# Graph attention on one core: GpSimd multiplies three tiles of V per block, ScalarE sums the K·Q products of two

## The reference

```python
edge_index = jnp.stack([src, dst])
q = (x @ Wq + bq).reshape(n, H, DK)       # H = 8 heads, DK = 64
k = (x @ Wk + bk).reshape(n, H, DK)
v = (x @ Wv + bv).reshape(n, H, DK)
logits = jnp.einsum('ehd,ehd->eh', q[rows] * scale, k[cols]) + att_bias
row_max = jax.ops.segment_max(logits, rows, num_segments=n)
p = jnp.exp(logits - row_max[rows])
denom = jax.ops.segment_sum(p, rows, num_segments=n)
att = p / denom[rows]
y = jax.ops.segment_sum(att[:, :, None] * v[cols], rows, num_segments=n)
out = y.reshape(n, H * DK) @ Wo + bo
```

## Time and profile before

| | us |
|---|---|
| median of 3 runs | 3242.53 |
| lowest, highest | 3241.57, 3242.64 |
| the profiled execution, its own time | 3243.5 |
| its span, first to last instruction | 3241.7 |

### The profile page before, as it was taken

How to read it: one execution, slowest core, us unless ns; L and a number is a source line. 1 busy time by engine, 2 the same in 40 slices (tenths; PEclk the granted TensorE clock), 3 DMA queues, 4 the chain that set the end, 5 groups by cost and what they waited for, 6 DMA issues and landing times.

```text
span 3241.7 us, 62767 instructions
## 1 busy us (share of the span) xinstructions
PE 2890.7 (89%) x11939; PEld 1687.3 (52%) x11939; DVE 2847.3 (88%) x20435; ACT 2108.6 (65%) x7365; POOL 2263.5 (70%) x2562
## 2 busy tenths in 40 slices
PE   4899888888888278999999999999999999989998
PEld 3555554454555134555555555555555555554444
DVE  8997777767777378999999999999999999998887
ACT  8332222222222037999999999999999999974444
POOL 0477777777777746888888888888888888861121
PEclk6798899988888688999999999999999999999999
DMA  6343443433333487888888888888888888841222
GB/s 189 78 138 108 106 112 108 114 103 99 109 108 97 132 312 247 270 263 268 261 270 266 265 265 265 269 265 261 271 265 266 264 265 269 262 142 61 84 79 71
DMA packets 259601, 619.75 MB, mean 191 GB/s; under 512 B 62433, under 2 KB 80493, under 8 KB 258958
## 3 DMA queue, kind: packets, MB, share of 16 engines
q0 software_dynamic: 144832, 443.72, 43.6%
q1 hardware_dynamic: 110862, 164.95, 17.0%
q10 hardware_dynamic: 3520, 7.08, 0.6%
HBM read 553.68 MB, written 61.92 MB: 190 GB/s over the span
## 4 chain that ended last, share of the span: by engine, by line
DVE 46%; POOL 23%; issue 14%; PE 12%; DMA 2%; DVEq 1%; ACT 1%; SPq 0%; POOLq 0%
DVE big L1361 26%; POOL rec_scratch L673 23%; DVE big L1470 12%; PE banks L2024 5%; PE banks L2089 2%; DVEq L1470 1%; DVE big L1081 1%; DVE big L1455 1%; PE banks L2003 1%; PE banks L2012 1%; PE banks L1947 1%; DMA big<-kv_scratch,small 1%; DVE ext L1439 1%; PE banks L2092 1%; DMA big<-in_edge_attr_dram 1%
## 5 line engine op out<-in xcount | busy, mean ns | idle before, releaser
L886 ACT ACTIVATE big<-big,small 128x65 f32<-128x65 f32 x6164 | 1508.8, 340 | 5.1 <-DMA big<-kv_scratch,small 0.4
L1361 DVE SCALAR_TENSOR_TENSOR big<-banks,big 128x64 f32<-128x64 f32 x6656 | 1030.6, 214 | 35.8 <-PE banks L1947 18.0
L694 POOL DMA_INDIRECT big<-kv_scratch,small x832 | 844.5, 1015 | 280.7 <-DVE big L1361 133.0
L673 POOL DMA_INDIRECT rec_scratch<-big,small x782 | 773.7, 989 | 324.5 <-issue 237.9
L1947 PE MATMUL banks<-big,small 128*128 x1664 | 892.7, 619 | 44.2 <-DVE big L1361 35.0
L2003 PE MATMUL banks<-big,small 128*128 128x260 f32 x3328 | 882.9, 388 | 44.3 <-DVE big L1470 22.1
L2003 PEld LDWEIGHTS banks<-big,small 128*128 128x128 f32 x3328 | 616.3, 190 | 449.7 <-issue 289.9
L1470 DVE SCALAR_TENSOR_TENSOR big<-big,loS,banks 128x520 f32 x832 | 619.6, 745 | 6.3 <-PE banks L2003 4.1
L1838 PE MATMUL banks<-big 128*128 128x512 f32 (+1 forms) x1176 | 598.0, 656 | 22.2 <-DVE big L1071 22.2
L702 POOL TENSOR_SCALAR small<-iotaF,small 128x128 f32<-128x128 f32 x832 | 527.9, 635 | 65.8 <-PE banks L2003 39.0
L1361 DVE DVE_READ_ACCUMULATOR big<-banks,big 128x1 f32 x6656 | 522.7, 79 | 0.1
(11 more groups left out here) (274 smaller groups left out, 2733.7 us busy)
## 6 DMA issues: line engine op xcount, KB each, us to landing
rowR<-lo_rows SPq DMA_DIRECT2D x97, 256.0 KB
big<-src_rows SPq DMA_DIRECT2D x97, 256.0 KB
big<-in_x_dram SPq DMA_DIRECT2D x96, 256.0 KB, 4.1
big<-kv_scratch,small POOLq DMA_INDIRECT x832, 5.3
rec_scratch<-big,small POOLq DMA_INDIRECT x782
kv_scratch<-big SPq DMA_DIRECT2D x48, 260.0 KB
q_scratch<-big SPq DMA_DIRECT2D x48, 256.0 KB
kv_scratch<-big SPq DMA_DIRECT2D x48, 256.0 KB
```

Of the source, the lines that this page charges most:

```text
L673: e.indirect_dma_start(recd, bass.IndirectOffsetOnAxis(ap=ridx[:, c % 4, j:j + 1], axis=0), rec[:, 8 * c + j, :], None).then_inc(s_sc[c % ...
L694: e.indirect_dma_start(KV[:, vat(t):vat(t) + YW + D], None, KVd, bass.IndirectOffsetOnAxis(ap=recB[b_ % 4][:, t % 16, 9:10].bitcast(i32), ...
L886: ins = e.activation(heads(Vr(t), h, h + 1), heads(Vr(t), h, h + 1), ACT.Copy, scale=ph[:, h:h + 1])
L1361: ins = e.scalar_tensor_tensor(k_, QB[t % 2][:, 64 * h:64 * h + 64], 1.0, k_, ALU.mult, ALU.mult, accum_out=Lr[t // 16 % 2][:, t % 16, h:h ...
```

## The change

`on_pool` now names tiles 6, 10 and 14 of each block instead of tile 10 alone. POOL multiplies V of such a tile in step s = t+25, right ahead of the tile's one-hot, where before it was four steps earlier and behind a one-hot. ACT leaves these tiles out, so it has no `pva` in steps 13, 1 and 5.

For tiles 3 and 9 of each block (`summed`; 99 tiles) DVE multiplies K by Q with one instruction of 512 columns and no sums. ACT makes the sums with the new `sums(t)`: eight copies in place of 64 columns with an accumulator output, in step t+3 (steps 6 and 12), ahead of the `pva` of that step. `gather(s)` now waits also for the sums of tile s-5, since it writes over that product; the block's `lb` (adding the bias) waits for them too. The semaphore that counts the sums is `s_ab` taken on from the sorting.

```diff
-        on_pool = [t % 16 in (10,) and t < LAST for t in range(T)]
+        summed = [t % 16 in (3, 9) and t < LAST - 16 for t in range(T)]
+        sum_at = [sum(summed[:t + 1]) for t in range(T)]
+        s_sum, sum_base = s_ab, 2 * NCH
+        on_pool = [t % 16 in (6, 10, 14) and t < LAST for t in range(T)]
...
                 q.wait_ge(s_rd, k + 1)
+                if k >= 0:
+                    q.wait_ge(s_sum, sum_base + sum_at[k])
                 q.wait_ge(s_yt, v + 1)
...
                 if s - DEL - 2 >= 0:
+                    if on_pool[s - DEL - 2]:
+                        pvp(s - DEL - 2)
                     one_hot(s - DEL - 2)
-                if 0 <= s - DEL + 2 < T and on_pool[s - DEL + 2]:
-                    pvp(s - DEL + 2)
...
+            def sums(t):
+
+                q.wait_ge(s_rd, t + 1)
+                q.wait_ge(s_x2, t // 16 - 1)
+                for h in range(8):
+                    k_ = Kr(t)[:, 64 * h:64 * h + 64]
+                    ins = e.activation(k_, k_, ACT.Copy, accum_out=Lr[t // 16 % 2][:, t % 16, h:h + 1])
+                ins.then_inc(s_sum, 1)
...
+                if 3 <= s < T + 3 and summed[s - 3]:
+                    sums(s - 3)
                 if s >= DEL and not on_pool[s - DEL]:
                     pva(s - DEL)
...
+                if summed[t]:
+                    if not half:
+                        e.tensor_tensor(Kr(t), QB[t % 2], Kr(t), ALU.mult).then_inc(s_rd, 1)
+                    return
...
                 q.wait_ge(s_rd, 16 * b_ + 16)
+                q.wait_ge(s_sum, sum_base + sum_at[16 * b_ + 15])
```

## The result

The changed kernel takes 3441.51 us (median of four runs, 3438.78 to 3446.75), beside 3242.05 for the kernel before in the same comparison: 1.062 times, 95% interval 1.061 to 1.063. It is slower, as forecast, and 45 us beyond the forecast of 3396 us. The profiled execution has a span of 3440.3 us.

What follows compares the result with a forecast made beforehand. DVE bounds the kernel, with ACT and PE within 4%. The ring's terms sum to 35.95 us a block against 32.7, +3.2 us over 48 blocks, 154 us on 3243.5, giving 3396 us by the median; range 3265 to 3480 us.

Steps and rivals of the forecast that it cites:

- The bound and the mechanism: DVE full before; afterwards tile 14's gather waits for ACT's sums of tile 9, a 2.4 us stall against 1.1 saved.
- 3 or 4: Sign in the profile: ACT's wait ahead of the copy of one-hots stays or grows to 3 or 4 us a block.
- the ring: Chain from one gather of tile 14 to the next through POOL, DVE, PE and ACT: 35.95 us a block against 32.7.
- gather 14 to gather 0: POOL's steps from gather 14 to 15 (1.84 us) and 15 to 0 (2.85 us, with a product of V): 4.7 us.
- gather 0 to tile 0: Landing of gather 0, after which DVE starts tile 0: 5.3 us.
- tile 0's start to tile 2's end: DVE from the start of tile 0 to the end of tile 2: 5.65 us.
- from there to gather 14, with both sums: Via PE to ACT's step 4 3.05 us, ACT to step 12 15.1, tile 9's sums 1.95, semaphore 0.2.
- the pointer that is not read: ACT's sums priced like `pva`, which reads a pointer where sums have an accumulator: 0.243 us a head, 1.95 a tile.
- The lag of ACT behind tile 9: ACT starts the sums 3.35 us after tile 9's product, 4.4 us with DVE 1.1 us ahead by its savings.
- rival "not slower": ACT's sums come in time; POOL's 32.5 us bounds a block, 3230 us, or DVE's 31.6, 3189 us; chance 0.10.
- The length of the sums enters twice: Tile 3's and tile 9's sums lie on one ACT stretch: at 1.2 us a tile a block takes 34.4, at 2.7 37.4.
- ACT is never idle up to step 12: From the copy of step 4 ACT works without waits, 15.1 us to step 12, `pva` 5 exchanged for tile 3's sums.

Runs made afterwards that it cites:

- e5: Changed kernel, but ACT sums tile 3 in step 5 and tile 9 in step 10 instead of 6 and 12; 1.013 times the kernel before, block 33.7 us.
- e1: Changed kernel without sums on ACT, so only POOL's three products of V a block; 1.026 times the kernel before, block 34.6 us.
- e4: Changed kernel, but POOL multiplies tile 15 in place of tile 14; 1.073 times the kernel before, block 38.0 us.
- e8: Changed kernel, but ACT sums only tile 3 and DVE sums tile 9 itself; 1.023 times the kernel before, block 34.5 us.
- e3: Changed kernel with an added summing copy of 16 columns ahead of each of ACT's sums; 1.100 times the kernel before, block 39.7 us.
- e9: Changed kernel, but ACT sums only tile 9; 1.069 times the kernel before, block 37.4 us.
- e11: Against the kernel before: ACT sums only tile 2 (step 4), POOL multiplies tiles 5 and 10; 3226.35 us against 3242.67, 0.994 times.

## Why the prediction was right, and where it was not

**The bound and the mechanism** were right. DVE stopped being full, POOL waits for ACT's sums at the gather of tile 14, DVE for its landing, and ACT's wait ahead of the copy of step 4 grew from 1.25 to 3.9 us, the "3 or 4" of the forecast. e5 shows that it is the sums' place in ACT's order: moved two tiles up, 3.2 of the 4.2 us are gone. The six blocks in which the wait falls on the gather of tile 15, and which are 1.8 us shorter, point the same way.

**The terms of the ring**, a block of the change beside the forecast, means over the blocks of its trace:

| term | forecast | measured |
|---|---|---|
| gather 14 to gather 0 | 4.7 | 5.0 |
| gather 0 to tile 0 | 5.3 | 4.8 |
| tile 0's start to tile 2's end | 5.65 | 6.2 |
| from there to gather 14, with both sums | 20.3 | 20.9 |
| sum | 35.95 | 36.9 |

- The kernel took 45 us more than the forecast of 3396 us: the ring is 0.95 us a block longer, over 48 blocks. Three terms were too short by 0.3, 0.5 and 0.6 us and one too long by 0.5, which brought the sum nearer than its parts were; that much is luck.
- Gather 14 to gather 0 is longer by the six blocks in which the wait stands between gathers 14 and 15. Gather 0 landed sooner than the median of 5.3 us.
- A set of sums lasts 1.91 us (forecast 1.95). The price was right by luck, for the wrong reason: I took it from the pointer that is not read, and in fact a second instruction of 188 ns follows each copy, half hidden, and both together come to 0.24 us a head. The 0.2 us for the semaphore had no row behind it; in the change 0.21 us pass from the end of tile 9's sums to the gather.
- The lag of ACT behind tile 9 was 3.8 us (forecast 4.4). The gather of tile 14 went out 6.6 us after the product in the 36 blocks in which it is the one that waits (forecast 6.5), and tile 14 started 4.7 us after it (forecast 4.4).
- Tile 0 to tile 2 was too short by 0.5 us: tile 1 follows its own gather there (5.3 us after it), not DVE's pace. I let POOL decide for tile 0 only.
- The stretch of ACT was taken as free of waits between steps 4 and 12. It holds one, 0.4 to 0.5 us at the copy of step 8; that is most of the 0.6 us in the last term.

**What was missing** is the contention. The forecast counted for POOL's two more products only POOL's own time and the late one-hots. Each of them can hold up a DVE instruction by a microsecond: 1.0 us a block in the change at line 1449. In e1, where DVE is the bound, it is the whole loss. What it costs in the change is not shown. The ring passes DVE at tile 2, ahead of it, and the terms of the table make up the whole block without it, so most of it should be hidden there; part may stand in the wait at step 8. e4 was to measure it and did not. The rival "not slower" put POOL's load alone at 32.5 us a block, 3230 us. Without the late sums the kernel would have been slower all the same, 1.023 to 1.026 times (e8, e1); that rival had failed on both of its terms.

**"The length of the sums enters twice"** held for longer sums but for 0.4 us (e3: 2.75 us for 2 x 1.6). It failed for shorter ones (e9: nothing gained). The step of the forecast behind it was that from the copy of step 4 on "ACT is never idle up to step 12"; this is so only as long as ACT comes to step 8 later than PE, and in the change it comes 0.4 us earlier on average.

## What to carry to other kernels

When work goes from a full engine to one with time to spare, look not at how much time that engine has but where in its order the new work stands, and who waits for its result: here the sums behind two products of V instead of ahead of them cost 3.2 us a block. A wait on an engine with an in-order queue delays all that is queued behind it, so a transfer that had 3 us to spare is the thing to check first. And GpSimd is not free time beside a full VectorE either: here each meeting of its product of V with a VectorE instruction that has both inputs in SBUF cost up to a microsecond, so such meetings belong in the count.

## What the runs showed of the hardware

- A product of two SBUF inputs on POOL (1.07 us) holds up a DVE instruction with two SBUF inputs until its end, even one on 8 partitions and one column (1.23 us for 0.2), and even when that one's record starts 0.14 us ahead. In e1 the prolonged instructions of lines 1390 and 1432 end 0.16 and 0.02 us behind the product, in 41 of 52 blocks each. DVE's K times Q (0.214 us) and its sum for Y (0.74 us), each with an input in PSUM, keep their durations within 10 ns beside it, and POOL's one-hots (one tensor input) leave line 1369 at 0.29 us.
- The issue of a gather on POOL (1.02 us) holds up such a DVE instruction too, by up to 0.27 us. In e11 the 8x17 instruction of line 1425 lasts 0.23 us by itself; in the 32 blocks in which it starts 0.28 to 0.45 us into a gather it lasts 0.3 to 0.5 us and ends 0.77 us after the gather's start each time.
- ACT's summing copy is two instructions, ACTIVATE of 241 ns and ACTIVATION_READ_ACCUMULATOR of 188 ns for 64 columns, and one head follows the other after 0.24 us, so about as fast as a copy with a scale from a pointer (0.243 us).
- A gather that goes out after a pause lands faster: tile 14 starts 4.7 us after it on average, where the median landing is 5.3 us.
